# A two-layer graph network with top-p attention on one core: resident halves, ties dropped by place, a root on VectorE, and a mask ahead of a branch

## The reference

```python
# layer 0: quantised graph convolution
support = relu(quant4(h) @ quant3(normalised W)) ; support_q = quant4(support)
x = x + adj @ support_q
# layer 1, with h = relu(layernorm(x)); X = h, Xf = Xa = h, Z = 0
R = (adj + I) / rowsum(adj + I)
for s in range(2):
    logits = (Xa @ W1) @ W2 @ (Xa @ W3).T              # 2048 x 2048
    # top-p 0.9: sort each row, keep the largest values up to and including the
    # one at which the cumulated softmax passes 0.9, softmax over the kept ones
    A = softmax(where(keep, logits, -inf))
    Xf = R @ Xf ; Xa = A @ Xa
    Z = Z + Xf @ U1[s] + Xa @ U2[s]
x = x + layernorm(X + Z) * gamma + beta
```

## Time and profile before

| | |
|---|---|
| runs | 1532.55, 1529.28, 1532.36 us; median 1532.36 |
| profiled execution: its own time, its span | 1530.33 us, 1528.5 us |
| busy: PE, DVE, ACT, POOL | 82%, 75%, 39%, 18% of the span |
| chain that ended last, by engine | PE 45%, DVE 26%, issue 14%, ACT 6%, DMA 3%, POOL 3% |
| ACT L943, exponential of a tile | 32 of 1990 ns mean |
| ACT L958, eviction of a tile of R @ Xf | 32 of 685 ns mean |
| DVE L1208, search pass over a tile | 146 of 2437 ns mean |
| VR and XR loads | 2 each, 4096 KB |

### The profile page before, as it was taken

The page is one execution under the profiler, slowest core; times in us unless marked ns, Lnnn a source line. Parts: engine busy times, 40 slices in busy tenths (PEclk is TensorE's granted clock), DMA queues, the critical chain, the costliest instruction groups (busy, mean ns, idle before and its releaser), DMA issues.

```text
span 1528.5 us, 18985 instructions
## 1 busy us (share of the span) xinstructions
PE 1253.8 (82%) x6522; PEld 617.6 (40%) x6522; DVE 1141.0 (75%) x1972; ACT 603.1 (39%) x1137; POOL 272.3 (18%) x231
## 2 busy tenths in 40 slices
PE   0458999994898699899899996699799369999995
PEld 0224555541343354445455552244344134445442
DVE  7976566653998998898798302897798999589456
ACT  1323444437611544554532435800444054443231
POOL 3212343330132020211221200010010001011011
PEclk9889999998999799999999999799899789999998
DMA  6224655647143011211201005343111102122235
GB/s 213 82 93 164 229 210 205 240 162 271 55 137 135 11 63 37 75 44 40 97 28 56 36 23 196 133 137 124 49 57 36 67 21 70 42 70 69 99 118 184
DMA packets 62069, 159.64 MB, mean 104 GB/s; under 512 B 5856, under 2 KB 5856, under 8 KB 57632
## 3 DMA queue, kind: packets, MB, share of 16 engines
q1 hardware_dynamic: 61984, 158.64, 29.5%
HBM read 99.11 MB, written 59.51 MB: 104 GB/s over the span
## 4 chain that ended last, share of the span: by engine, by line
PE 45%; DVE 26%; issue 14%; ACT 6%; DMA 3%; POOL 3%; SPq 1%; DVEq 1%; POOLq 0%; ACTq 0%
PE AB L738 13%; PE AB L741 6%; DVE WS L1208 6%; PE UB L606 5%; PE RB L706 5%; PE AB L596 4%; PE TB L615 3%; DVE turns L1164 3%; DMA AD<-z_d 2%; PE RB L708 2%; ACT squares L923 2%; PE XB L606 1%; POOL RT L503 1%; DVE E L1364 1%; DVE w L1393 1%
## 5 line engine op out<-in xcount | busy, mean ns | idle before, releaser
L1208 DVE SCALAR_TENSOR_TENSOR WS<-E,g 128x2048 bf16<-128x2048 f32 x146 | 348.4, 2437 | 3.0 <-issue 1.7
L738 PE MATMUL AB<-XR,turns 128*128 128x512 f16 x1024 | 244.5, 382 | 0.0
L706 PE MATMUL RB<-VR,turns 128*128 128x512 f16 x1024 | 234.5, 379 | 0.0
L1293 DVE TENSOR_REDUCE g<-E 128x1 f32<-128x2048 f32 x32 | 72.9, 2278 | 110.8 <-ACT E L916 110.4
L706 PEld LDWEIGHTS RB<-VR,turns 128*128 128x128 f16 x1024 | 100.0, 98 | 111.3 <-issue 0.6
L738 PEld LDWEIGHTS AB<-XR,turns 128*128 128x128 f16 x1024 | 101.0, 99 | 108.6 <-issue 4.9
L741 PE MATMUL AB<-XR,turns 128*128 128x512 f16 x512 | 131.4, 379 | 0.0
L978 ACT ACTIVATE turns<-TB 128x512 f16<-128x512 f32 x128 | 75.3, 594 | 130.6 <-PE TB L621 130.5
L503 POOL TENSOR_TENSOR RT<-RT,AD 128x512 f32<-128x512 f32 x32 | 56.6, 1768 | 350.6 <-ACT RT L958 350.6
L708 PE MATMUL RB<-VR,turns 128*128 128x512 f16 x512 | 117.7, 379 | 0.0
L606 PE MATMUL UB<-UW,XT 128*128 128x512 f16 x384 | 88.2, 379 | 27.9 <-ACT XT L867 27.7
(11 more groups left out here) (253 smaller groups left out, 1965.1 us busy)
## 6 DMA issues: line engine op xcount, KB each, us to landing
turns<-adj_parts SPq DMA_DIRECT2D x64, 512.0 KB, 3.7
E<-adjT SPq DMA_DIRECT2D x16, 1024.0 KB, 5.9
adj_parts<-turns SPq DMA_DIRECT2D x16, 1024.0 KB, 6.4
x_parts<-XHL SPq DMA_DIRECT2D x32, 256.0 KB, 3.0
v_parts<-VHL SPq DMA_DIRECT2D x32, 256.0 KB, 2.0
VR<-v_parts SPq DMA_DIRECT2D x2, 4096.0 KB, 13.8
XR<-x_parts SPq DMA_DIRECT2D x2, 4096.0 KB, 24.2
z_d<-UO SPq DMA_DIRECT2D x31, 256.0 KB, 2.0
```

Source lines behind the costliest of these rows:

```text
L706: i = mm(RB[:, :], AT[:, 0, j, :], VR[:, j, k % 2, :], start=False, stop=False)
L738: mm(AB[:, :], ET[:, 0, j, :], XR[:, j, y_, :], start=(j == 0 and y_ == 0), stop=False)
L1208: return v.scalar_tensor_tensor(junk[t % 2], e, g4[:, k, t:t + 1], e, op, ALU.mult, accum_out=g4[:, F_, t:t + 1])
L1293: ct(v.tensor_reduce(row(A2)[:, t:t + 1], E[:, slot, :], AX.X, ALU.max))
```

## The change

Six edits in one.

- **Resident halves.** In layer 0 ACT and POOL write the halves into `XR[t]` and `VR[t]` themselves; the stores to `x_parts` and `v_parts` and the loads at the head of step 0 go. For step 1 the halves still go by DRAM: `VR` is loaded ahead of the last group's pairs of step 0 (`v_in`), `XR` at the head of step 1 (`x_in`).
- **One tile of R @ Xf earlier.** `r_tile` does tile 0 between the logits of group 0 and of group 1, in both steps; `r_tiles` starts at 1.
- **Root on VectorE.** POOL's `terms` go; four short instructions on DVE make twice the root (a first value from the bits, one Newton step), and the constants that use it are halved.
- **Ties by place.** POOL makes once, at the start, a row of 1 to 2048 as float16 (`order`, in the space of gamma and beta, whose loads move to the last group). A flagged tile then takes three long passes: the places of the entries equal to the threshold, the eight largest places, and the dropping of those beyond. `rank_equals` is left only behind the bisection, which has one more condition: that the last entry of the window of eight is within the slack of the threshold (and that entries are to be dropped).
- **First mask ahead of the branch.** The mask of the group's first tile is issued ahead of the read of the flags, with a threshold `SAFE`, which is zero in rows that a flag names. If any flag is set, that tile is masked again in the branch.
- **One reciprocal for a group**, behind its four masks; ACT's scaling waits on `s_rden` instead of `s_kept`.

```diff
-        gam = sb("gam", [P, D], F32)
-        bet = sb("bet", [P, D], F32)
+        gb = sb("gb", [P, 2, D], F32)
+        gam, bet = gb[:, 0, :], gb[:, 1, :]
+        order = gb[:, :, :].rearrange("p a d -> p (a d)").bitcast(F16)
@@ step_order
             logits(s, 0)
             terms(s, 0)
+            r_tile(s)
             logits(s, 1)
             r_tiles(s)
@@ SP
-            sp.dma_start(gam[:, :], gamma.partition_broadcast(P)).then_inc(s_gb, 16)
-            sp.dma_start(bet[:, :], beta.partition_broadcast(P)).then_inc(s_gb, 16)
             def post0_stores(t):
-                x_store(t, t)
                 sp.wait_ge(s_ue, t + 1 + OPEN)
                 sp.dma_start(xu10_d[t], UO[:, :]).then_inc(s_uout, 16)
-                sp.wait_ge(s_vl, t + 1 + OPEN)
-                sp.dma_start(v_parts[t], VHL[:, :, :]).then_inc(s_vout, 16)
+            def r_tile(s):
+                if s == 0:
+                    at_hi_in(s, 0)
+                    at_lo_in(s, 0)
+                ad_in(s, 0)
+                if s:
+                    x_in()
             def pairs(s, g):
+                if s == 0 and g == NG - 1:
+                    v_in()
+                    at_hi_in(1, 0)
+                    at_lo_in(1, 0)
                 if last:
+                    sp.wait_ge(s_kept, 2 * T)
+                    sp.dma_start(bet, beta.partition_broadcast(P)).then_inc(s_gb, 16)
+                    sp.dma_start(gam, gamma.partition_broadcast(P)).then_inc(s_gb, 16)
@@ POOL
+            q.memset(order[:, 0:1], 1.0).then_inc(s_order, 1)
+            for k in range(LOG_N):
+                pool.wait_ge(s_order, k + 1)
+                q.tensor_scalar(order[:, 2 ** k:2 ** (k + 1)], order[:, 0:2 ** k], 2.0 ** k, None,
+                                ALU.add).then_inc(s_order, 1)
-            def terms(s, g):
-                pool.wait_ge(s_gvar, s * NG + g + 1)
-                q.tensor_tensor(g4[:, SIG, :], g4[:, VAR, :], powc[:, 1, 0:G], ALU.pow).then_inc(s_gsig, 1)
@@ DVE, first_guess
-                v.tensor_scalar(row(VAR), row(VAR), 1e-12, None, ALU.max).then_inc(s_gvar, 1)
-                dve.wait_ge(s_gsig, gq + 1)
+                    ct(v.tensor_scalar(row(VAR), row(VAR), 1e-12, None, ALU.max))
+                    ct(v.tensor_scalar(row(SIG).bitcast(I32), row(VAR).bitcast(I32), 0.5, ROOT, ALU.mult, ALU.add))
+                    ct(v.reciprocal(row(A2), row(SIG)))
+                    ct(v.tensor_tensor(row(A2), row(A2), row(VAR), ALU.mult))
+                    ct(v.tensor_tensor(row(SIG), row(SIG), row(A2), ALU.add))
@@ DVE, settle
+            def in_order(e, t):
+                v.scalar_tensor_tensor(WS[:, :], e, g4[:, THR, t:t + 1], order, ALU.is_equal, ALU.mult)
                 v.drain()
+                v.max(h8[:, t, :], WS[:, :])
+                v.drain()
+                v.scalar_tensor_tensor(h8[:, t, :], order[:, 0:WIN], g4[:, BAD, t:t + 1], h8[:, t, :], ALU.is_ge, ALU.mult)
+                v.drain()
+                v.tensor_reduce(row(A1)[:, t:t + 1], h8[:, t, :], AX.X, ALU.max)
+                v.drain()
+                v.scalar_tensor_tensor(e, WS[:, :], row(A1)[:, t:t + 1], e, ALU.is_le, ALU.mult)
+                v.drain()
+                ct(v.tensor_tensor(row(A1), row(A1), h8[:, :, WIN - 1], ALU.max))
                 ct(v.scalar_tensor_tensor(row(A1), row(BAD), 1.5, row(A1), ALU.is_gt, ALU.mult))
+                ct.free(v.scalar_tensor_tensor(row(SAFE), flag[:, 5:9], 0.0, row(THR), ALU.is_equal, ALU.mult))
+                masked(tiles[0][0], 0, SAFE)
                 any_flag = dve.value_load(total[0:1, 0:1].bitcast(I32))
                 with dve.If(any_flag != NEVER):
+                    v.drain()
                     for slot, t in tiles:
                         with dve.If(dve.value_load(total[0:1, 1 + t:2 + t].bitcast(I32)) != NEVER):
                             bisect(E[:, slot, :], t)
+                            rank_equals(E[:, slot, :], t)
+                            v.memset(g4[:, BAD, t:t + 1], 1.0)
+                            v.drain()
                         with dve.If(dve.value_load(total[0:1, 5 + t:6 + t].bitcast(I32)) != NEVER):
-                            rank_equals(E[:, slot, :], t)
-                        keep(slot, t)
+                            in_order(E[:, slot, :], t)
+                        masked(slot, t, THR).then_inc(s_kept, 1)
                 with dve.If(any_flag == NEVER):
-                    for slot, t in tiles:
-                        keep(slot, t)
+                    v.drain()
+                    dve.sem_inc(s_kept, 1)
+                    for slot, t in tiles[1:]:
+                        masked(slot, t, THR).then_inc(s_kept, 1)
+                dve.wait_ge(s_kept, G * gq + G)
+                ct(v.reciprocal(row(A1), row(DEN)))
+                v.tensor_scalar(rden[:, sl], row(A1), 1.0 / SE, None, ALU.mult).then_inc(s_rden, 1)
```

More of the change, by code:

```diff
@@ L538, in pairs @@
                     tile(s, g, i)
[L540 to L541 removed]
+            step_order(0, nothing, nothing, r_tile, r_tiles, pairs, r_sum)
+            step_order(1, nothing, nothing, r_tile, r_tiles, pairs, r_sum)
         @block.tensor
@@ L1057, in pairs @@
                     tile(s, g, i)
-            step_order(0, logits, terms, r_tiles, pairs, r_out)
-            step_order(1, logits, terms, r_tiles, pairs, r_out)
+            step_order(0, logits, terms, r_tile, r_tiles, pairs, r_out)
+            step_order(1, logits, terms, r_tile, r_tiles, pairs, r_out)
         @block.vector
```

160 lines of the change are left out of this document (86 added, 74 removed).

## The result

| | before | changed |
|---|---|---|
| median of the runs | 1531.43 us (1529.28 to 1532.55, 4 runs) | 1479.3 us (1478.89 to 1480.17, 4 runs) |
| span of the profiled execution, mean granted clock | 1528.5 us, 0.947 | 1477.1 us, 0.963 |

Before the change a fourth run, of 1530.5 us, has joined the three. The ratio is 0.9663, with a 95% interval of 0.9648 to 0.9678. The forecast was 1481.5, the range 1471 to 1497.

What follows compares the result with a forecast made beforehand. It took PE's idle stretches, chiefly behind one long VectorE chain in step 1, as the bound. 1 - 4.9 - 43.8 - 2.1 = -49.8 us against 1530.3 gave 1480.5, plus 1 for a median: 1481.5, range 1471 to 1497.

Steps and rivals of the forecast that it cites:

- step 1: Up to PE's return at 1232.40: tile 0 in PE's hole, root and cheaper settling of flagged tiles save 43.8 us.
- Start: Before layer 0: POOL's eleven instructions for `order` delay the quantisation's power, +1 us, bounds 0 to 6.3.
- nearer the memset: At the start: one-input additions for `order` cost nearer a memset than a two-input subtraction, hence only +1 us.
- Layer 0: Loop of layer 0: nobody waited for the stores that go, so 0, with 1 us allowed either way.
- Step 0, first group: VectorE's chain before PE's return at 507.90: masks, root and less contention save 4.9 us.
- contention -1.0: Step 0, first group: tile 0's POOL work moves beside ACT's exponentials, away from VectorE's passes, saving 1.0 us.
- Rest of step 0: Groups of step 0 behind PE's return: PE ends last there, so nothing is gained, 0.
- The root: VectorE's 1.19 us wait for POOL replaced by four short instructions: -0.3 or -0.4 in step 0's guesses, -0.9 in step 1.
- Behind the return: After PE's return in step 1: -2.1 us, 1.5 from a better clock after a short rest, 0.6 from a wait at 1349.36.
- Rival 1: Step 1: the tile moved into PE's hole gives nothing, gain 31.6 us there, time 1493.7; chance 0.08.
- Rival 3: A tie at the window's last entry sends a tile to bisection, 186 us more on step 1's chain, 1667; chance 0.05.
- Rival 4: All terms, from start to layer 0, come at their good ends: 1475.8 us; chance 0.08.

Runs made afterwards that it cites:

- experiment 2: Changed kernel with tile 0 of R @ Xf back behind the second group's logits in both steps: 1493.13 us.
- experiment 3: Changed kernel with flagged tiles ordered by the old running sums (`rank_equals`) instead of by places: 1510.57 us.
- experiment 1: Changed kernel with POOL building the row of places behind its subtractions of the weights, not at the start: 1477.52 us.
- experiment 8: Changed kernel that also stores layer 0's halves to DRAM again, with nobody reading them: 1480.7 us.
- experiment 10: Kernel before the change with one edit, the root of the variance on VectorE instead of POOL: 1526.68 us.
- experiment 9: Changed kernel with the row of places built later and tile 0 of R @ Xf ahead only in step 1: 1478.06 us.
- experiment 4: Changed kernel with the root of the variance back on POOL, one power for four tiles: 1491.13 us.
- experiment 11: Changed kernel with ACT's high half of the R @ Xf tile behind two chunks of terms, at heads of step 0's groups 1 and 2: 1471.55 us.
- experiment 6: Changed kernel with the loads of VR and of the first tile of `adj_parts` back at the head of step 1: 1481.36 us.
- experiment 12: Changed kernel with both the row of places built later and ACT's high half later at step 0's groups 1 and 2: 1472.55 us.

## Why the prediction was right, step by step

**What bounds the kernel, and step 1: right.** Of the 51.4 us, 43.5 came in the stretch that the prediction named, for 43.8 predicted. The logits' start to the first search pass shortened by 13.0 us (-12.2 predicted), the flagged settling by 30.9 (-31.6). Experiments 2 and 3 undo one part each and lose 13.8 and 31.3. The first mask hid most of the read, as counted: 1.19 us of idle is left before the second (1.91 in step 0).

**Start: mis-sized, +4.4 for +1.** The step that failed is "nearer the memset". Eleven dependent instructions over 2,047 elements took 8.30 us, inside the bounds of 4.0 to 10.3 but at the far half. The fixed part was near its lower bound (the shortest one took 0.22 us, the median one 0.29), but the last, over 1024 elements, took 2.77 us, more for each element than the two-input subtraction. The side estimate of 1.8 us for the eleven, worked out from the Trainium skill ("GPSIMD Engine Reference", section 3.1), does not hold in this trace either. The late row of experiment 1 shows 3.1 us of it come back.

**Layer 0: 0 for -4.4.** "I allow 1 us either way" was too narrow. That nobody waited for the stores was right (experiment 8). What was overlooked is that an edit moves every instruction of POOL against VectorE's by a fraction of a microsecond. PE's 0.20 us of a tile most likely hung on this, 2.4 us in all, and another 1.4 are the clock of the last tile, which experiment 10 has without the resident halves. In experiment 10, which has none of this change in layer 0, the stretch took 252.82 us, 3.4 less than before, behind a start 4.1 later: single profiles of the first two stretches can't be split more finely than that.

**Step 0, first group: -2.6 for -4.9.** The masks gave nearly what was counted: from the last transpose to the next maximum it is 12.51 us (to 486.30) for 15.77 (to 488.60), 3.3 less. Another 0.35 came before the first pass of the search and 0.3 behind the maxima, where the prediction had 0.7 for the root. The step that failed is "contention -1.0": tile 0's sum did not land beside ACT's exponentials but in the search itself, and from the first pass to the last transpose it took 1.3 us more, not less, 0.4 of it the two short instructions that were added. POOL's two instructions and the two short ones of VectorE that met them, in the changed kernel:

```profile
385.21 1.56 POOL L518 TENSOR_TENSOR RT<-RT,AD 128x512 f32<-128x512 f32 x1 [32.66 <-ACT RT L982]
385.58 1.22 DVE L1360 TENSOR_SCALAR g<-tot 128x4 f32<-128x4 f32 x1
...
387.51 3.10 POOL L494 TENSOR_TENSOR VHL<-RT,VHL 128x512 f16<-128x512 f32 x1 [0.74 <-ACT VHL L986]
...
389.64 0.99 DVE L1367 TENSOR_TENSOR gi<-g 128x8 int32<-128x8 f32 x1
```

By experiment 9 the tile ahead is worth 0.5 in this step at most. The sign "idle in step 0 down from 14.69 to about 10" failed too: it is 21.19, since the prediction left out that the tile ahead also ends PE's work sooner (12.34 with the tile behind, experiment 9).

**Rest of step 0: 0 for -3.9.** "In the other groups PE ends last and nothing is gained" failed. PE stood 3.54 us at the heads of groups 1 and 2, and the root of VectorE took 1.06 off each, by letting POOL's sum begin at another point of a pass. Experiment 4 loses 4.6 us in this stretch and experiment 10 gains 2.3, so by experiment 4 the root accounts for all of it, by experiment 10 for 2.3. Experiment 11 shows that more was to be had at the same two places.

**The root: mis-sized.** The prediction took one wait, the 1.19 us of the earlier trace rows, for all groups. The view of waits of before has all of them:

```profile
DVE g L1306 <- POOL g L497: 34.2, 8, 11.8
```

It was 34.2 us over eight, with single ones of 2.54, 6.87, 8.36 and 11.77. Of the 11.8 us that experiment 4 gives to the root, 1.6 were forecast. That the sum is within 2.2 us of the median owes something to luck: by the table the terms missed by +3.4, -4.4, +2.3, -3.9, +0.3 and +0.8, which nearly cancel.

**Behind the return: -1.35 for -2.1.** The granted clock was 1.00 for 0.75, and 1.31 of the 1.35 are in the first stretch behind the return (11.31 us for 12.62). That a short rest alone gives the whole clock is refuted: in experiments 6, 11 and 12 PE returned behind waits of 2.60 to 2.85 us, as here behind 2.79, and was granted 0.81 or 0.82 over 8 us. The 1.65 us at 1349.36 and their ordinary 1.03 gave nothing that stays.

**The rivals.** Rival 1 (the tile gives nothing) and 2 (ordering stays dear) are what experiments 2 and 3 built: 1493.1 and 1510.6 for 1493.7 and 1510. Rival 3 is out, since the search pass ran 144 times and no bisection came. Rival 4, all terms at their good ends, did not come: the start went the other way.

## What to carry to other kernels

When an instruction goes from one in-order engine to another, take the sum of the waits for it over all groups from the view of waits, not the one wait that stands on the critical path. When ACT waits for another engine only to make something that nobody needs soon, put the waiting instruction behind the evictions that the busiest engine needs: here that gave 7.8 us. Where two engines disturb each other, the difference of a few microseconds between two builds can come from their meeting 0.1 us earlier or later, so a part that was not touched is to be bounded by such meetings, not by nothing. And two neighbouring stretches of one profile can trade such a difference, so compare several profiles before a stretch is given a cause.

## What the runs showed of the hardware that was not expected

In these rows VectorE and POOL don't share; one waits for the other to end. A sum of POOL takes 1.26 us alone. Begun 0.10 us behind a pass of 2.34 us it took 3.36, begun 1.18 behind it took 2.29: both ended 1.1 us after the pass. The other way round a 1.23 us instruction of VectorE begun 0.04 us behind POOL took 5.09 us. A short one of VectorE beside POOL took 0.99 to 1.29 for 0.16 to 0.23. The Trainium skill has this as a rule ("SBUF — State Buffer", "Who interferes with whom"): the pair of ports is an exclusive lock, and who issues first keeps it for the whole instruction. These rows agree. The prediction had used the rule only as a price per tile, while what it decides is order: the same two instructions cost 0.3 us of POOL or 4 us of VectorE.

A row of numbers doubled in eleven dependent instructions of POOL took 8.30 us, while a memset of the same width took 1.80. Most of it is not the number of instructions: the median one took 0.29 us, the last, over 1024 float16 elements, 2.77.
